# Attention and routed feed-forward on one core: two self iterations in one bank, eleven iterations a unit, pieces in new places

## The chip, the cores and the metric

The kernel runs on one core of a Trainium2 chip. The time is device microseconds of one execution, from its first to its last instruction on the core, with what lies around them. TensorE (PE) multiplies matrices, VectorE (DVE) and ScalarE (ACT) work on 128 partitions, GpSimd (POOL) does light work beside them, SyncE (SP) issues DMAs. The program is written by hand, engine by engine, with semaphores.

## The reference

Eight batches of 512 tokens with 256 channels, and a context of 1024 tokens for each:

```python
scale = np.float32(1.0 / np.sqrt(D))                      # 16 heads of D = 16
q = _heads(x @ Wq + bq); k = _heads(x @ Wk + bk); v = _heads(x @ Wv + bv)
att = jnp.einsum('bhqd,bhkd->bhqk', q, k) * scale
att = jnp.where(causal[None, None], att, -jnp.inf)
y = jnp.einsum('bhqk,bhkd->bhqd', jax.nn.softmax(att, axis=-1), v)
qc = _heads(x @ Wcq + bcq); kc = _heads(cross_input @ Wck + bck); vc = _heads(cross_input @ Wcv + bcv)
attc = jnp.einsum('bhqd,bhkd->bhqk', qc, kc) * scale
y = y + jnp.einsum('bhqk,bhkd->bhqd', jax.nn.softmax(attc, axis=-1), vc)
...
x = x + xattn(_layernorm(x), ctx)
x = x + ffn(_layernorm(x))    # gate, top 512 tokens for each of 8 experts, LN, fc1, gelu, fc2, weight, scatter-add
```

## The kernel before

`attention` computes the first line of the two; `feed_forward`, a second block behind it, the other. The change is in `attention` alone.

**Units and iterations.** A batch has four units (`UNITS`) of four heads. In a unit the scores are computed keys by queries: iterations 0 to 7 (`CROSS_IT`) take one tile of 128 context keys each, against 512 queries; iterations 8 to 11 one tile of 128 own keys each, against the 512, 384, 256 and 128 queries that may see it (`score_span`). For every head of an iteration PE makes scores in a PSUM bank (L577), ACT takes the exponential into `probs` (L784), POOL zeroes the forbidden corner of self tiles (L1084), and PE multiplies by the values into `out_ps` (L593, `values`). `probs` has two buffers, so the values of an iteration are multiplied at the end of the next. When the cross or the self part of a unit is complete, ACT copies `out_ps` out (`copy_out`, L796).

**Maxima.** The softmax shift of a row is its largest score. PE makes the scores a second time, queries by keys (L614), and DVE reduces them: over 512 context keys (L871), or with the causal mask (L874). A unit has 48 of these (`N_A`), four an iteration (`A_PER_IT`), made 68 maxima (`LEAD`) ahead of the unit's scores. `finish_maxima` and the piece "shift" turn them into two rows that are laid beside q by DMA (`put_shift`).

**Two halves of the array.** q and k are kept as high and low parts, stacked: each head uses 64 of the 128 partitions (`SIDE`). Heads 0 and 2 stand in the lower half, 1 and 3 in the upper, so a score matmul of one half can run beside one of the other. Scores go upper, lower (`for side in (1, 0)`), maxima lower, upper by their number.

**Banks.** Three PSUM banks (`SCORE_BANKS`) go round among scores and pieces, four (`RING`) among maxima and the pieces that DVE consumes (`by_vector`: out and proj). PE waits in `bank_free` until the last user of a bank is done.

**Pieces.** All other work of the attention (projections q, qc, k, kc, v, vc of the next batches, transposes, output projection, norm, gate) is cut into pieces. The table `PLAN` says at which (unit, iteration) each stands; PE, ACT, DVE and POOL all walk through the same table. In an iteration PE's order is: maximum, two scores, maximum, pieces, maximum, two scores, maximum, values of the iteration before. For a q, qc, k or kc piece ("half piece", names in `COL`), PE multiplies, ACT writes the rounded high part (L821), DVE subtracts it from the bank for the low part (`low_half`, L929) and so frees the bank, SP stores both to DRAM (`store_parts`) and loads the stacks of a unit from there (`fill`).

**Start.** DVE and POOL clear `q_stack` and `k_stack` (L992, L995, L1001; L1113, L1115), POOL presets `v_self` and `v_cross` (L1116, L1117); DVE normalizes the first tokens (L998), PE transposes them and makes the first ten half pieces, SP fills the stacks of units 0 and 1 directly (`fill_directly`, L462). Then PE and DVE make `LEAD` maxima, and the batches begin.

## Time and profile before

| | us |
|---|---|
| median of 3 runs | 1687.46 (1686.04 to 1691.6) |
| profiled execution, its own time | 1687.51 |
| its span | 1685.8 |
| start, up to the first maximum | 0 to 46.5 |
| first maxima | 46.5 to 88.2 |
| batches with their epilogue | 88.2 to about 1315 |
| feed-forward | about 1315 to 1685.8 |

The span is cut by the first and last instructions of each stage. Within the batches a unit lasts 35 to 41 us, 32 of them stand in a row. Matmul durations overlap: what one costs the engine is the distance of its start to the next start. A group's idle time is that of its own engine; DVE, ACT and POOL have idle time all along the batches, and only such of it counts as ends in a wait of PE.

### The profile page before, as it was taken

To read this page: it belongs to the slowest core of one execution; us is meant where nothing else is said; L and a number is where in the kernel's file an instruction comes from. 1 tells how busy PE (TensorE), PEld (TensorE's weight loads), DVE (VectorE), ACT (ScalarE), POOL (GpSimd) and SP (SyncE) were. 2 spreads that over 40 slices of the span, in tenths; PEclk is the share of its full clock that TensorE was granted. 3 is DMA by queue.
4 is the path that set the end of the run, shared out by engine and by line. 5 is a ranking of instruction groups with operands and counts; after the bars stand their busy time and mean duration, and the time that the engine had idled before them with its cause. 6 is when DMAs were issued, how large, how long until landed. Compare 5 with 4: busy or idle time off the path is not lost. (4 is left out here: it accounts for less than half of the span.)

```text
span 1685.8 us, 26485 instructions
## 1 busy us (share of the span) xinstructions
PE 1524.3 (90%) x8921; PEld 723.5 (43%) x8921; DVE 1190.5 (71%) x3234; ACT 920.4 (55%) x1882; POOL 422.0 (25%) x859
## 2 busy tenths in 40 slices
PE   5799999999999999999999999999999525999997
PEld 2443343444344434444443444334333312665564
DVE  7778887887888788778877887887880165555441
ACT  2067777677766677676777677677767100112111
POOL 4021131322132113212231322131131301343342
PEclk7689999999999999899999999999999656999999
DMA  3673772765285547636671855376200210444432
GB/s 87 155 132 90 131 92 71 110 119 104 79 121 110 95 90 126 112 84 100 120 116 66 122 100 100 89 122 116 34 3 3 70 48 14 116 90 109 116 82 50
DMA packets 82492, 155.47 MB, mean 92 GB/s; under 512 B 13012, under 2 KB 46420, under 8 KB 82356
## 3 DMA queue, kind: packets, MB, share of 16 engines
q1 hardware_dynamic: 76212, 145.25, 44.4%
q0 software_dynamic: 6144, 8.52, 2.9%
q8 instruction: 71, 1.16, 0.3%
q14 instruction: 65, 0.53, 0.1%
HBM read 96.52 MB, written 53.08 MB: 89 GB/s over the span
## 5 line engine op out<-in xcount | busy, mean ns | idle before, releaser
L784 ACT ACTIVATE probs<-bank_ps 128x512 f32<-128x512 f32 (+3 forms) x1536 | 743.3, 545 | 277.9 <-PE bank_ps L577 271.7
L871 DVE TENSOR_REDUCE chunk_max<-bank_ps 128x1 f32<-128x512 f32 x1024 | 646.8, 681 | 88.7 <-PE bank_ps L614 86.3
L577 PE MATMUL bank_ps<-q_stack,k_stack 64*128 64x512 f32 (+3 forms) x1536 | 542.2, 432 | 33.4 <-ACT probs L784 26.8
L614 PE MATMUL bank_ps<-k_stack,q_stack 62*128 62x512 f32 (+3 forms) x1536 | 560.0, 441 | 10.6 <-DMA k_stack<-parts 5.1
L614 PEld LDWEIGHTS bank_ps<-k_stack,q_stack 62*128 62x128 f32 x1536 | 254.0, 190 | 390.1 <-DVE chunk_max L871 177.0
L577 PEld LDWEIGHTS bank_ps<-q_stack,k_stack 64*128 64x128 f32 x1536 | 237.3, 187 | 117.0 <-ACT probs L784 101.1
L593 PE MATMUL out_ps<-probs,v_cross 128*32 128x512 f32 x2048 | 272.7, 605 | 0.0
L874 DVE CUSTOM_DVE_ANT_0 masked<-bank_ps,causal 128x128 bf16<-128x128 f32 (+3 forms) x512 | 232.2, 485 | 30.5 <-PE bank_ps L614 26.5
L1035 POOL TENSOR_TENSOR pool_idle<-pool_idle 128x1 f32<-128x1 f32 x287 | 55.4, 193 | 599.1 <-ACT probs L784 429.7
L1317 ACT ACTIVATE h<-h_ps,b1T 128x512 f32<-128x512 f32 x64 | 44.0, 687 | 269.5 <-PE h_ps L1270 138.5
L1284 PE MATMUL o_ps<-w2T,h 128*128 128x256 f32 x512 | 115.4, 382 | 14.2 <-DVE o L1425 7.2
L1075 POOL TENSOR_TENSOR y_sb<-y_sb,y_add 128x256 f32<-128x256 f32 x32 | 23.3, 728 | 415.1 <-DVE y_add L917 415.1
L1270 PE MATMUL h_ps<-ff_yT,w1T 128*128 128x512 f32 x256 | 122.9, 616 | 1.0 <-DVE ff_yT L1330 1.0
L929 DVE SCALAR_TENSOR_TENSOR parts<-bank_ps,bias,parts 128x512 fp32r<-128x512 f32 x75 | 56.2, 750 | 80.4 <-ACT parts L821 80.2
L1284 PEld LDWEIGHTS o_ps<-w2T,h 128*128 128x128 f32 x512 | 95.5, 190 | 35.5 <-issue 13.3
L1084 POOL TENSOR_SCALAR_AFFINE_SELECT probs<-probs 128x256 f32<-128x256 f32 x256 | 104.2, 407 | 0.0
L593 PE MATMUL out_ps<-probs,v_self 128*32 128x512 f32 (+3 forms) x1024 | 98.0, 457 | 0.0
L821 ACT ACTIVATE parts<-bank_ps,bias 128x512 fp32r<-128x512 f32 x75 | 51.6, 688 | 58.5 <-PE bank_ps L630 54.8
L593 PEld LDWEIGHTS out_ps<-probs,v_cross 128*32 128x32 f32 x2048 | 40.3, 108 | 76.4 <-issue 52.1
L1523 POOL TENSOR_TENSOR ff_pool_idle<-ff_pool_idle 128x1 f32<-128x1 f32 x48 | 12.9, 268 | 213.8 <-DVE index_next L1378 129.5
L1270 PEld LDWEIGHTS h_ps<-ff_yT,w1T 128*128 128x128 f32 x256 | 46.0, 193 | 39.9 <-issue 39.5
L1368 DVE TENSOR_SCALAR onehot<-iota,e_row 128x128 bf16<-128x128 bf16 x256 | 44.3, 253 | 11.6 <-PE list_ps L1258 11.5
(157 smaller groups left out, 1344.5 us busy)
## 6 DMA issues: line engine op xcount, KB each, us to landing
parts_dram<-parts SPq DMA_DIRECT2D x70, 512.0 KB, 2.7
k_stack<-parts_dram SPq DMA_DIRECT2D x180, 192.0 KB, 11.5
q_stack<-parts_dram SPq DMA_DIRECT2D x180, 128.0 KB, 10.5
w1T<-in_L_ffn_fc1s SPq DMA_DIRECT2D x8, 1024.0 KB, 5.7
w2T<-in_L_ffn_fc2s SPq DMA_DIRECT2D x8, 1024.0 KB, 7.3
z_rows<-z_sb SPq DMA_DIRECT2D x8, 528.0 KB, 3.0
x_sb<-in_x SPq DMA_DIRECT2D x8, 512.0 KB, 4.0
ctxT<-in_ctx SPq DMA_DIRECT2D x8, 512.0 KB, 5.3
```

Source lines behind the costliest of these rows:

```text
L577: pe.matmul(bank_of(turn)[:, q0:T], k_stack[base:base + SIDE, g, pair, kc:kc + P], q_stack[base:base + SIDE, g, pair, qc + q0:qc + T], sta ...
L593: mm = pe.matmul(out_ps[32 * h:32 * h + 32, q0:T], v[:, g // 2, kt, g % 2 * UH + h, :], probs[:, i % 2 * 2 + h // 2, h % 2, q0:T], start=k ...
L614: return pe.matmul(bank[:, 0:n], q_stack[base:base + MAX_ROWS, g, pair, qc:qc + P], k_stack[base:base + MAX_ROWS, g, pair, k0:k0 + n], sta ...
L784: nc.scalar.activation(probs[:, i % 2 * 2 + p, side, q0:T], bank_of(("score", g, i, p, side))[:, q0:T], ACT.Exp, scale=SCALE)\
L821: nc.scalar.activation(parts_of(piece)[:, 0], bank[:], ACT.Identity, bias=bias[:, BIAS[name], hf:hf + 1]).then_inc(high_done, 1)
L871: nc.vector.tensor_reduce(dst, bank[:, 0:n], AX.X, ALU.max).then_inc(max_done, 1)
L874: nc.vector.tensor_tensor_reduce(masked[:, a % 2, 0:n], bank[:, 0:n], causal[:, T - n:T], 1.0, LOWEST, ALU.add, ALU.max, dst).then_inc(max ...
L929: nc.vector.scalar_tensor_tensor(out=parts_of(piece)[:, 1], in0=bank[:], scalar=bias[:, BIAS[name], hf:hf + 1], in1=parts_of(piece)[:, 0], ...
L1035: nc.gpsimd.tensor_tensor(pool_idle[:, c:c + 1], pool_idle[:, 0:1], pool_idle[:, 0:1], ALU.add)
L1084: nc.gpsimd.affine_select(out=tile, in_=tile, pattern=[[0, 2], [1, P]], compare_op=ALU.is_ge, fill=0.0, base=0, channel_multiplier=-1).the ...
L1270: mm = pe.matmul(h_ps[:, f % 2], w1T[:, k, f * P:(f + 1) * P], yT[:, k, :], start=k == 0, stop=k == KT - 1)
L1284: mm = pe.matmul(o_ps[:, t % 2, 0:C], h[:, f, t * P:(t + 1) * P], w2T[:, f, :], start=f == 0, stop=f == FT - 1)
```

## The change

- The last two self tiles, 256 and 128 queries wide, share a bank (`score_spans`): two score matmuls per head, one exponential over 384 columns, both masks behind it. A unit has 11 iterations (`ITS`), the last is the joined one.
- The 48 maxima of a unit stand as 4 in iterations 0 to 6 and 5 in 7 to 10 (`A_AT`). With five, three stand ahead of the pieces and two behind (`ahead_of_pieces`).
- `probs` gets a third pair of buffers; PE multiplies the values of an iteration two iterations later (`BEHIND`), ACT's `copy_out` moves one iteration back.
- Half pieces of batches 1 to 7 (70 of 80): ACT writes the unrounded value once, which frees the bank (`whole_done`); POOL rounds a copy and subtracts it (`split_halves`). DVE's part goes. SP waits for POOL (`halves_ready`).
- `PLAN` is rewritten: shift in iteration 7, not 8; k, kc0, kc1, qc, q, gate and others one to three iterations away from where they stood.
- Start: DVE clears the last three quarters of `q_stack` behind the normalization, in one; POOL clears the rest of `k_stack` only when the normalization is done; pair 0 of unit 0 is filled with q and k before pair 1; six warm-up matmuls, not four.

```diff
-ITS = 12
-A_PER_IT = 4
-N_A = ITS * A_PER_IT
+SELF_ITS = 3
+ITS = CROSS_IT + SELF_ITS
+A_AT = (4, 4, 4, 4, 4, 4, 4, 5, 5, 5, 5)
+A_FROM = tuple(itertools.accumulate(A_AT, initial=0))
+N_A = A_FROM[ITS]
...
+BEHIND = 2
+PROB_BUFFERS = BEHIND + 1
...
-    (2, 6): (("vc0", 0),), (2, 8): (("shift", 0),), (2, 9): (("qc", 1),), (2, 11): (("k", 1),),
+    (2, 6): (("vc0", 0),), (2, 7): (("shift", 0),), (2, 8): (("qc", 1),), (2, 10): (("k", 1),),
...
-            for pair in range(UH // SIDES):
-                fill_directly(0, pair, True, first_in[pair])
+            fill_directly(0, 0, True, first_in[0])
             sp.wait_ge(*freed(prologue_piece(PROLOGUE.index(("kc1", 0)))))
-            for pair in range(UH // SIDES):
-                fill_directly(0, pair, False, first_in[pair])
+            fill_directly(0, 0, False, first_in[0])
+            fill_directly(0, 1, True, first_in[1])
+            fill_directly(0, 1, False, first_in[1])
...
+            if i < ITS - 1:
+                return [self_span(i - CROSS_IT, (i - CROSS_IT) * P)]
+            return [self_span(SELF_ITS - 1, 0), self_span(SELF_ITS, T - (SELF_ITS - 1) * P)]
...
                         maxima(0)
                         score_pair(b, g, i, 0, first, last)
-                        maxima(1)
+                        for n in range(1, ahead_of_pieces(i)):
+                            maxima(n)
...
-                        maxima(2)
+                        maxima(A_AT[i] - 2)
                         score_pair(b, g, i, 1, first, last)
-                        maxima(3)
-                        if not (first and g == 0 and i == 0):
-                            values(*before)
+                        maxima(A_AT[i] - 1)
+                        done = ITS * (UNITS * b + g) + i - BEHIND
+                        if done >= 0:
+                            values(done // (ITS * UNITS), done // ITS % UNITS, done % ITS)
...
-                    nc.scalar.activation(parts_of(piece)[:, 0], bank[:], ACT.Identity,
-                                         bias=bias[:, BIAS[name], hf:hf + 1]).then_inc(high_done, 1)
+                    if piece.of > 0:
+                        nc.scalar.activation(parts_of(piece)[:, 1].bitcast(F32), bank[:], ACT.Identity,
+                                             bias=bias[:, BIAS[name], hf:hf + 1]).then_inc(whole_done, 1)
...
-                elif piece.name in COL:
+                elif piece.name in COL and piece.of == 0:
                     low_half(piece, bank)
...
-            nc.vector.memset(q_stack[:, 1].bitcast(F32), 0.0).then_inc(q_clear, 1)
             dve.wait_ge(rstd_step[0], 2)
...
-            nc.vector.memset(q_stack[:, 2:4].bitcast(F32), 0.0).then_inc(q_clear, 1)
+            nc.vector.memset(q_stack[:, 1:4].bitcast(F32), 0.0).then_inc(q_clear, 1)
...
+            def split_halves(piece):
+
+                a, e = COL[piece.name]
+                n = number_of(piece) - 2 * len(HALF_PIECES) + 1
+                pool.wait_ge(whole_done, n)
+                hold()
+                nc.gpsimd.tensor_copy(parts[:, 0, a:e], parts[:, 1, a:e].bitcast(F32)).then_inc(rounded, 1)
+                pool.wait_ge(rounded, n)
+                nc.gpsimd.tensor_tensor(parts[:, 1, a:e], parts[:, 1, a:e].bitcast(F32), parts[:, 0, a:e].bitcast(F32),
+                                        ALU.subtract).then_inc(split_done, 1)
...
             deviation(0, 1)
+            pool.wait_ge(ln_done[0], 1)
             nc.gpsimd.memset(k_stack[:, 1:4].bitcast(F32), 0.0).then_inc(k_clear, 1)
```

**SP at the start**, the direct fills of units 0 and 1; before:

```order
17 L425 DMA gateT<-in_L_ffn_gate_w 128x16
18 L462 DMA q_stack<-parts 16x1024 x12
19 L462 DMA k_stack<-parts 16x1536 x12
20 L462 DMA q_stack<-parts 16x1024 x6
21 L462 DMA k_stack<-parts 16x1536 x6
```

and now:

```order
17 L447 DMA gateT<-in_L_ffn_gate_w 128x16
18 L484 DMA q_stack<-parts 16x1024 x6
19 L484 DMA k_stack<-parts 16x1536 x6
20 L484 DMA q_stack<-parts 16x1024 x6
21 L484 DMA k_stack<-parts 16x1536 x6
```

Six q fills, those of pair 1, have moved behind the six k fills of pair 0.

**PE at the end of unit 3**, from values to values; L614 are maxima, L577 scores, L593 values. Before, the 128-wide iteration, with its two scores of each pair between maxima:

```order
1109 L593 MATMUL out_ps<-probs,v_self 32x384 x4
1110 L614 MATMUL bank_ps<-k_stack,q_stack 128x384
1111 L577 MATMUL bank_ps<-q_stack,k_stack 128x128 x2
1112 L614 MATMUL bank_ps<-k_stack,q_stack 128x384
1113 L614 MATMUL bank_ps<-k_stack,q_stack 128x512
1114 L577 MATMUL bank_ps<-q_stack,k_stack 128x128 x2
1115 L614 MATMUL bank_ps<-k_stack,q_stack 128x512
1116 L593 MATMUL out_ps<-probs,v_self 32x256 x4
```

and now the joined one (L655 maxima, L616 scores, L634 values):

```order
1117 L655 MATMUL bank_ps<-k_stack,q_stack 128x512
1118 L616 MATMUL bank_ps<-q_stack,k_stack 128x256
1119 L616 MATMUL bank_ps<-q_stack,k_stack 128x128
1120 L616 MATMUL bank_ps<-q_stack,k_stack 128x256
1121 L616 MATMUL bank_ps<-q_stack,k_stack 128x128
1122 L655 MATMUL bank_ps<-k_stack,q_stack 128x384 x2
1123 L655 MATMUL bank_ps<-k_stack,q_stack 128x512
1124 L616 MATMUL bank_ps<-q_stack,k_stack 128x256
1125 L616 MATMUL bank_ps<-q_stack,k_stack 128x128
1126 L616 MATMUL bank_ps<-q_stack,k_stack 128x256
1127 L616 MATMUL bank_ps<-q_stack,k_stack 128x128
1128 L655 MATMUL bank_ps<-k_stack,q_stack 128x512
```

A fifth maximum has come in, and each head has two score matmuls in a row on its half of the array.

**POOL around the first half pieces of a batch** (unit 0 into unit 1), before:

```order
193 L1035 TENSOR_TENSOR pool_idle<-pool_idle 128x1
194 L1084 AFFINE_SELECT probs<-probs 128x2x128
195 L1075 TENSOR_TENSOR y_sb<-y_sb,y_add 128x4x64
196 L1035 TENSOR_TENSOR pool_idle<-pool_idle 128x1
197 L1084 AFFINE_SELECT probs<-probs 128x2x128
```

and now:

```order
217 L1081 TENSOR_TENSOR pool_idle<-pool_idle 128x1
218 L1142 AFFINE_SELECT probs<-probs 128x2x128 x2
219 L1081 TENSOR_TENSOR pool_idle<-pool_idle 128x1
220 L1129 CAST parts<-parts 128x512
221 L1131 TENSOR_TENSOR parts<-parts 128x512
222 L1081 TENSOR_TENSOR pool_idle<-pool_idle 128x1
223 L1129 CAST parts<-parts 128x512
224 L1131 TENSOR_TENSOR parts<-parts 128x512
```

Between the masks of a unit and its `y_sb` addition POOL now has a copy and a subtraction for each half piece.

## Rows read from the trace of the kernel before

**Rows 1.** The page, part 1: busy us, share of the span, instructions.

```profile
PE 1524.3 (90%) x8921; PEld 723.5 (43%) x8921; DVE 1190.5 (71%) x3234; ACT 920.4 (55%) x1882; POOL 422.0 (25%) x859
```

**Rows 2.** Engines by stretch: length, then busy us of each, PEclk, DMA.

```profile
88.20:1315.00 1226.80, 1187.85 (x7527) 510.32 (x7527) 953.91 (x2372) 861.05 (x1795) 287.87 (x690) 0.98 0.53 95
```

**Rows 3.** Timeline, DVE at the start: start us, us, instruction, count, idle before.

```profile
8.71 13.58 DVE L998 TENSOR_SCALAR x_sb<-x_sb,mean_var,rstd 128x256 f32<-128x256 f32 x4
```

**Rows 4.** Line L998 alone: durations ns min/median/max.

```profile
L998 DVE TENSOR_SCALAR x_sb<-x_sb,mean_var,rstd x4: 395/400/12619, 8.7 to 21.9; 128x256 f32<-128x256 f32 x4
```

**Rows 5.** Timeline, POOL at the start.

```profile
8.22 7.77 POOL L1115 MEMSET k_stack<- 128x9216 f32 x1
...
17.67 3.50 POOL L1117 MEMSET v_cross<- 128x4096 f32 x1
```

**Rows 6.** Timeline, PE at the start.

```profile
22.43 1.94 PE L625 MATMUL bank_ps<-ident,x_sb 128*128 128x128 f32 x8 [15.11 <-DVE x_sb L998]
25.14 3.75 PE L630 MATMUL bank_ps<-y0T,w_q 128*128 128x512 f32 x4 [0.77 <-ACT y0T L813]
28.69 2.39 PE L630 MATMUL bank_ps<-y0T,w_cq 128*128 128x512 f32 x4
30.91 1.88 PE L630 MATMUL bank_ps<-y0T,w_k 128*128 128x512 f32 x4
...
46.48 0.51 PE L614 MATMUL bank_ps<-k_stack,q_stack 62*128 62x512 f32 x1 [5.10 <-DMA k_stack<-parts]
```

**Rows 7.** Timeline, SP's DMA issues at the start.

```profile
32.69 7.58 SPq L462 DMA_DIRECT2D q_stack<-parts  x12
40.31 7.55 SPq L462 DMA_DIRECT2D k_stack<-parts  x12
```

**Rows 8.** Timeline, PE in batch 4, unit 2: iteration 2 (w_q) and iteration 3 (no piece).

```profile
792.79 0.50 PE L614 MATMUL bank_ps<-k_stack,q_stack 62*128 62x512 f32 x1
...
793.45 1.06 PE L593 MATMUL out_ps<-probs,v_cross 128*32 128x512 f32 x8
794.45 0.50 PE L614 MATMUL bank_ps<-k_stack,q_stack 62*128 62x512 f32 x1
...
795.73 0.49 PE L577 MATMUL bank_ps<-q_stack,k_stack 64*128 64x512 f32 x1 [0.21 <-ACT probs L784]
...
796.15 1.07 PE L593 MATMUL out_ps<-probs,v_cross 128*32 128x512 f32 x8
```

**Rows 9.** Timeline, all engines behind a q piece, batch 4, unit 0 into unit 1.

```profile
744.20 0.69 ACT L821 ACTIVATE parts<-bank_ps,bias 128x512 fp32r<-128x512 f32 x1 [1.49 <-PE bank_ps L630]
744.92 0.75 DVE L929 SCALAR_TENSOR_TENSOR parts<-bank_ps,bias,parts 128x512 fp32r<-128x512 f32 x1 [1.53 <-ACT parts L821]
745.20 0.49 PE L614 MATMUL bank_ps<-k_stack,q_stack 62*128 62x512 f32 x1
745.82 0.50 PE L577 MATMUL bank_ps<-q_stack,k_stack 64*128 64x512 f32 x2
```

**Rows 10.** Timeline, PE in batch 3, unit 2, iteration 8 (shift, then late scores).

```profile
652.63 0.50 PE L614 MATMUL bank_ps<-k_stack,q_stack 62*128 62x512 f32 x1
653.13 0.99 PE L577 MATMUL bank_ps<-q_stack,k_stack 64*128 64x512 f32 x2
...
654.04 1.06 PE L593 MATMUL out_ps<-probs,v_cross 128*32 128x512 f32 x8
```

**Rows 11.** Timeline, POOL in batch 4, unit 2.

```profile
801.79 1.22 POOL L1053 TENSOR_SCALAR z_sb<-x,mean_var,rstd 128x256 f32<-128x256 f32 x1
803.09 2.37 POOL L1068 TENSOR_TENSOR x<-x,z_sb 128x1024 f32<-128x1024 f32 x1
```

**Rows 12.** Timeline, DVE at that time.

```profile
802.76 2.47 DVE L871 TENSOR_REDUCE chunk_max<-bank_ps 128x1 f32<-128x512 f32 x4
```

**Rows 13.** Engines by stretch, at the starts of batches 3 and 2.

```profile
548.30:554.50 6.20, 6.20 (x32) 4.08 (x31) 3.72 (x8) 3.75 (x7) 0.00 (x0) 0.50 0.75 152
394.00:400.20 6.20, 6.20 (x50) 3.57 (x49) 4.87 (x10) 5.14 (x10) 0.00 (x0) 1.00 0.75 163
```

More of the change, by code:

```diff
@@ L371, in bank_of, with buffer @@
             return bank_ps[:, SCORE_TURNS.index(turn) % SCORE_BANKS]
+        def buffer(u, i, pair):
+            return (ITS * u + i) % PROB_BUFFERS * 2 + pair
         def parts_of(piece):
@@ L430, in store_parts @@
                 a, e = COL[name]
[L431 removed]
+                sp.wait_ge(*halves_ready(piece))
                 if stacked and name == HALF_PIECES[0]:
```

107 lines of the change are left out of this document (65 added, 42 removed), and 13 rows, old and new, of the table PLAN.

## The prediction

> **What bounds the kernel now.** I read the busy shares first: PE is busy for 90% of the span, DVE for 71% [rows 1]. Then the stretches: the batches take 1226.8 us, and PE is busy for 1187.9 of them, at a granted clock of 0.98; DVE for 953.9, ACT for 861 [rows 2]. So the batches go by PE. But "busy" counts waiting in the pipeline as well, so the timeline has to say how much of it is work. It gives a price to each part of an iteration, from start to start: two maxima with two scores 0.66 us (792.79 to 793.45), four 512-wide value products 1.00 us (793.45 to 794.45) [rows 8]. An iteration without a piece is then worth 0.66 + 0.66 + 1.00 = 2.32 us, but takes 2.70 (793.45 to 796.15, values to values): 0.39 us stand in its second half, where the fourth score waits for ACT, since only three banks go round [rows 8]. This is a chain of latencies (score, exponential, bank), not anyone's load. The change leaves that chain as it is: three banks, same order.
>
> Such stalls can be counted through the batch. I find four kinds. (a) Behind a half piece DVE stands 1.53 us waiting for ACT's high part and then works 0.67 on the low part; PE has made one maximum at 745.20 and can go on only at 745.82, 0.6 us late [rows 9]. There are five such places a batch (behind q, qc, k of half 1, kc0, kc1), 2.8 us. (b) In the shift iteration the second half starts at 652.63 and the values at 654.04, 1.41 us where 0.66 would do [rows 10]: 0.75, four a batch, 3.0 us. (c) The iterations 9 to 11 wait some 0.2 to 0.4 each, 2.8 us a batch. (d) Iterations of context keys with no piece in a score or ring bank, 0.39 each [rows 8]; seven a batch.
>
> The start has bounds of its own. The first normalization on DVE takes 13.58 us for four small operations [rows 3]: the median of them is 0.40, one lasts 12.62 [rows 4]. It ends when POOL's last memset does: those run from 8.22 to 21.17 without a gap that matters [rows 5]. PE waits for it for 15.11 us [rows 6].
>
> **The change, part by part.**
>
> *Start.* (1) POOL's memsets wait for the normalization. It then costs 4 x 0.4 and begins at about 8.3: it ends near 10.0 and not at 22.3, a gain of 12.3 [rows 3, 4]. The Trainium skill (SBUF — State Buffer, Who interferes with whom) has this as a lock which the one that issues first holds for the whole instruction; the trace has the wait through three memsets in a row, not one, and the sum is the same by both. (2) q and qc took 3.75 and 2.39 where k took 1.88 [rows 6], because PE had stood idle; with six warm-up matmuls and a gap of about 1 us the clock should be at its upper level: 2.3 less. The last half piece of the start ends at about 26.9 instead of 41.4. (3) SP may begin the direct fills when `k_stack` is clear: 10.0 + 7.77 [rows 5] = 17.8, where it began at 32.69 [rows 7]. Pair 0 now needs six q issues (half of 7.58) and six k issues (half of 7.55) [rows 7]: 17.8 + 7.6 = 25.4, and 2.8 for the landing (from the issue at 40.31 + 3.4 to the first maximum at 46.48 [rows 6, 7]): 28.2. Both PE and DVE are done with the pieces by then. The first maximum moves from 46.48 to about 28.3: **-18 us**. DVE runs the maxima behind it at its own pace, so all of it stays. Ends: if PE gets the lower clock for all ten half pieces (3.75 each as the first one), the fills are no longer what ends last, and 10 are left; -19 if the first maxima also run smoother.
>
> *Half pieces.* DVE's wait and work (2.2 us, 70 times) go, and ACT's one write frees the bank. The stalls (a) go: -2.8 a batch. ACT's part costs what it did. POOL gets a copy and a subtraction of 512 columns. No row shows such a copy; memset gives the lower end (7.77 / 9216 x 512 = 0.4 us [rows 5]), the two-operation form the upper (1.22 for 256 columns [rows 11], 2.4). The subtraction is 2.37 / 2 = 1.2 [rows 11]. So 1.6 to 3.6 us, say 2.6, ten times in 152 us, on an engine busy for 288 of 1227 us [rows 2]. The masks stand behind it in POOL's queue; their consumer on PE now comes two iterations later, 5 us and more. SP's stores come 2 to 4 us later, while the fill with the least slack (half 0 into unit 0's stacks) has some 12 us between its landing and its first maximum. Price: 0, as long as that cover holds.
>
> *Eleven iterations.* The number of scores and maxima by columns is the same; an iteration's overhead goes. ACT saves four exponentials a unit, but is not the bound. The stalls (c) go with the sparse iterations 9 to 11, and shift (b) comes to an iteration with five maxima, so that PE works where it waited: -5.8 a batch. Two pieceless iterations of (d) are filled: -0.8. Against it: in an iteration with five maxima the alternation of the halves breaks. Before, a maximum and a score of different halves always go together, 0.33 us for both [rows 8]. Now one maximum stands alone, and at odd numbers (28 + 5 = 33) maximum and first score are on the same half. I count two unpaired slots a unit more than before: 8 x 0.336 = +2.7 a batch. The joined iteration has two score matmuls of one half behind each other, +0.4 a unit, +1.6. Pieceless self iterations still have the chain (d): four at 0.35, +1.4. `copy_out` now waits for values of 256 and 128 columns (0.57 + 0.36 us) instead of 128 alone: half of 0.57 shows, +1.1. Five reductions of 0.6 (2.47 for four [rows 12]) against an iteration of 2.9 to 3.2: +0.8. Sum: -9.4 + 7.6 = -1.8 a batch, **-14.4 us** for eight. The two values products left at the end cost +0.6.
>
> What same-half neighbours cost is not in this trace, since it has none. The nearest rows bound it: 0 if they overlap as opposite halves do, 0.336 if they do not at all [rows 8]. I take the upper end, since a pair starts in the same 0.01 us and the next pair only 0.34 later. The Trainium skill speaks against the change here (TensorE: Matmul & The Clock Gate, Part 3, The mechanism): the weight load runs beside matmuls in flight only if the row group differs. By it the +2.7 stand; by the other end the batches would gain 4.5 each.
>
> *Third buffer, values two behind.* PE waits for no mask or exponential ahead of its values now that would be worth a term, so this gives 0 by itself. It is the cover for POOL's new work.
>
> *Sum.* 1687.5 (the profiled execution, and the median to 0.1) - 18.0 - 14.4 + 0.6 = **1655.7 us**. The span would be 1654.
>
> **The rivals.**
>
> *R1, the halves do overlap, or the chain (d) shrinks where five maxima stand.* Then +2.7 and +1.4 fall away: 1656 - 8 x 3 = 1632 to 1640. For it: POOL and ACT have room. The clock works the same way: at the starts of batches 3, 4 and 5 it fell to the lower level for about 10 us. Beside the start of batch 2, 32 matmul records stand there instead of 50 in 6.2 us [rows 13]; the three falls cost about 6.5 us together. Ahead of them PE has sparse iterations (9 to 11 of unit 3), and these are denser now. Against it: the gate piece, eight-column matmuls, stays there.
>
> *R2, the batches gain nothing.* The new stalls (copy behind values, five reductions, unpaired slots) eat all 9.4: 1687.5 - 18 = 1669. For it: I have 7.6 of them from bounds, and at several places the values to values distance is PE's work already. The start stands by itself.
>
> *R3, the other side: slower.* POOL's split holds DVE. For the start the trace shows that DVE can stand for the whole of a POOL instruction [rows 3, 5]. If every split stopped the maxima for 2.6 to 3.6 us, against a slack of DVE in such an iteration of 4.0 - 4 x 0.6 = 1.6, this costs 1 to 2 us for each of 70: 1656 + 70 to 140 = 1726 to 1796, slower than before from 0.5 us a split upwards. Against it: while POOL runs 1.22 and 2.37 us operations that read and write SBUF, DVE's four maxima take 2.47 us as everywhere [rows 11, 12].
>
> *R4, the start gains less*, -10, with the batches as forecast or flat: 1664 to 1678.
>
> **How the numbers follow.** Forecast (1648 to 1663) 0.42, R1 0.23, R2 0.19, R4 0.10, R3 0.03, and 0.03 for something of another kind on the slow side. The predicted time is that of the forecast, 1656. From 1636 to 1676 it takes in forecast, most of R1, R2 and half of R4: about 0.8. About 0.3% (5 us) can be told from no change: faster than 1682.4 is 0.92; within 0.3% 0.04 (R4 with batches that lose 5 us); slower 0.04.
>
> **What would show each step.** Start: L998's successor at 0.4 us each, the first maximum at 28 to 29 us, first scores at about 70 instead of 88. If it is at 36, the clock of the half pieces was low. Batches: their stretch 1212 us instead of 1227. The five places (a): the score behind a maximum follows at once. Unpaired slots: in iterations 7 to 9, a maximum starting 0.33 us behind the other matmul of its half. The shift iteration at 3.2 us, as before, but full. POOL's copy and subtraction at 0.4 to 2.4 and 1.2 us, and maxima on DVE at 0.6 us apart beside them; if they stretch, R3 is right. I am wrong altogether if a fill lands late and PE waits for `slot_in` at the first maxima of a unit, or if the clock falls at many unit starts: each fall costs 2 to 3 us.

## The result and the profile after

The changed kernel takes 1622.4 us (median of 4 runs, 1616.12 to 1627.09), the kernel before 1689.23 beside it (4 runs). The ratio is 0.9603, with a 95% interval of 0.9565 to 0.9641: 67 us faster, where 32 had been forecast (1656, range 1636 to 1676). The sign was right, the size was not, and the time lies below the range.

The page after, part 1, answers to [rows 1]; behind it, in a fence of its own, the stretch of the batches (columns as in [rows 2]).

```profile
PE 1486.5 (92%) x8925; PEld 726.8 (45%) x8925; DVE 1135.0 (70%) x3163; ACT 911.5 (56%) x1754; POOL 550.1 (34%) x1005
```

```profile
69.10:1252.00 1182.90, 1153.28 (x7523) 516.38 (x7523) 909.74 (x2300) 852.30 (x1667) 415.87 (x836) 0.99 0.56 99
```

POOL has 128 us more to do than before, DVE 56 less, and PE's busy time has shrunk by 38 with about as many matmuls (8925 for 8921 [rows 1]): most of that is waiting inside PE's pipeline that has gone, since busy time counts it. By the first and the last exponential of the attention I cut both traces into three: the first exponential comes at 70.0 us where it came at 89.1 (-19.1), the batches from there to the last exponential take 1178.8 us where they took 1221.9 (-43.1), and what lies behind takes 372.9 where it took 374.8 (-1.9). The forecast had -18, -14.4 and +0.6. The batches are what was missed.

The start went as planned. Timeline of DVE, PE and SP there; the rows answer to [rows 3, 6, 7]:

```profile
8.35 1.38 DVE L1044 TENSOR_SCALAR x_sb<-x_sb,mean_var,rstd 128x256 f32<-128x256 f32 x4 [1.64 <-POOL rstd L1090]
11.75 3.55 PE L671 MATMUL bank_ps<-y0T,w_q 128*128 128x512 f32 x4 [0.82 <-ACT y0T L856]
15.14 1.88 PE L671 MATMUL bank_ps<-y0T,w_cq 128*128 128x512 f32 x4
18.63 3.78 SPq L484 DMA_DIRECT2D q_stack<-parts  x6
28.93 0.47 PE L655 MATMUL bank_ps<-k_stack,q_stack 62*128 62x512 f32 x1 [1.61 <-DVE u_sb L976]
```

The normalization takes 1.38 us instead of 13.58, the fills begin at 18.63, the first maximum stands at 28.93. What released it is DVE's last low half, not a fill.

POOL's new work in the middle of a batch (batch 4, unit 2 into unit 3), a copy and a subtraction of one half piece; behind it DVE's maxima in the same time, and the durations (ns, min/median/max) of all DVE maxima over 512 context keys:

```profile
777.73 0.61 POOL L1129 CAST parts<-parts 128x512 fp32r<-128x512 f32 x1
778.42 1.29 POOL L1131 TENSOR_TENSOR parts<-parts 128x512 fp32r<-128x512 f32 x1
```

```profile
777.27 1.29 DVE L918 TENSOR_REDUCE chunk_max<-bank_ps 128x1 f32<-128x512 f32 x2 [0.36 <-PE bank_ps L655]
```

```profile
L918 DVE TENSOR_REDUCE chunk_max<-bank_ps x1024: 656/681/694, 29.4 to 1200.2; 128x1 f32<-128x512 f32 x171
```

The copy takes 0.61 us, the subtraction 1.29. DVE's two maxima beside the copy take 1.29 us, half of the 2.47 for four in [rows 12], and none of the 1024 lasts longer than 0.694 us, though 70 copies and 70 subtractions stand among them. R3, POOL holding DVE, did not happen, though the start of the kernel before had shown a DVE operation standing through POOL's memsets [rows 4, 5]. The Trainium skill (SBUF — State Buffer, Who interferes with whom) tells the two apart: it names tensor_scalar, the normalization's operation, as one that can contend with GpSimd, and tensor_reduce, the maxima's, as one that never does on trn2. Both rows agree.

### The profile page after: what moved, and what is told of

It reads as the page before. It is cut to its first block and busy times, and to the rows that moved or that the text cites. A ratio compares the mean times of both kernels' runs of the same rounds, so it can differ in the third digit from the quotient of the medians.

```text
span 1621.7 us, 26374 instructions
## 1 busy us (share of the span) xinstructions
PE 1486.5 (92%) x8925; PEld 726.8 (45%) x8925; DVE 1135.0 (70%) x3163; ACT 911.5 (56%) x1754; POOL 550.1 (34%) x1005
## 5 line engine op out<-in xcount | busy, mean ns | idle before, releaser
L827 ACT ACTIVATE probs<-bank_ps 128x512 f32<-128x512 f32 (+1 forms) x1408 | 730.4, 579 | 247.2 <-PE bank_ps L616 238.5
L918 DVE TENSOR_REDUCE chunk_max<-bank_ps 128x1 f32<-128x512 f32 x1024 | 653.5, 683 | 143.4 <-PE bank_ps L655 139.6
L655 PE MATMUL bank_ps<-k_stack,q_stack 62*128 62x512 f32 (+3 forms) x1536 | 536.1, 432 | 7.7 <-DVE chunk_max L918 4.4
L616 PE MATMUL bank_ps<-q_stack,k_stack 64*128 64x512 f32 (+3 forms) x1536 | 511.7, 422 | 26.0 <-ACT probs L827 22.6
L655 PEld LDWEIGHTS bank_ps<-k_stack,q_stack 62*128 62x128 f32 x1536 | 248.2, 191 | 371.3 <-DVE chunk_max L918 201.6
L634 PE MATMUL out_ps<-probs,v_cross 128*32 128x512 f32 x2048 | 274.3, 608 | 0.0
L616 PEld LDWEIGHTS bank_ps<-q_stack,k_stack 64*128 64x128 f32 x1536 | 234.5, 189 | 83.9 <-ACT probs L827 76.5
L1131 POOL TENSOR_TENSOR parts<-parts 128x512 fp32r<-128x512 f32 x70 | 89.3, 1276 | 5.6
L634 PE MATMUL out_ps<-probs,v_self 128*32 128x512 f32 (+3 forms) x1024 | 90.4, 449 | 0.1
L634 PEld LDWEIGHTS out_ps<-probs,v_cross 128*32 128x32 f32 x2048 | 40.3, 108 | 76.7 <-issue 48.1
L865 ACT ACTIVATE parts<-bank_ps,bias 128x512 f32<-128x512 f32 x70 | 48.2, 689 | 46.6 <-PE bank_ps L671 43.5
L1612 POOL DMA_INDIRECT out<-o,index x32 | 50.7, 1584 | 5.2 <-issue 5.2
```

The costliest lines, as they stand in the source:

```text
L616: mm = pe.matmul(bank_of(turn)[:, of.at:of.end], k_stack[base:base + SIDE, g, pair, of.keys:of.keys + P], q_stack[base:base + SIDE, g, pai ...
L634: mm = pe.matmul(out_ps[32 * h:32 * h + 32, of.q0:T], v[:, g // 2, of.tile, g % 2 * UH + h, :], probs[:, buffer(u, i, h // 2), h % 2, of.a ...
L655: return pe.matmul(bank[:, 0:n], q_stack[base:base + MAX_ROWS, g, pair, qc:qc + P], k_stack[base:base + MAX_ROWS, g, pair, k0:k0 + n], sta ...
L827: nc.scalar.activation(probs[:, buffer(u, i, p), side, columns], bank_of(("score", g, i, p, side))[:, columns], ACT.Exp, scale=SCALE)\
L918: nc.vector.tensor_reduce(dst, bank[:, 0:n], AX.X, ALU.max).then_inc(max_done, 1)
L1131: nc.gpsimd.tensor_tensor(parts[:, 1, a:e], parts[:, 1, a:e].bitcast(F32), parts[:, 0, a:e].bitcast(F32), ALU.subtract).then_inc(split_don ...
```

## The experiments

The kernel before ran beside every group of them, at medians of 1686.5 to 1689.2 us. "Forecast" is the prediction's own theory; further theories are named where they came up.

Each median holds two things: how long the iterations last, and how long PE's granted clock was at the lower of its two levels. To tell them apart I add up a batch from the trace of each kernel: for every (unit, iteration) the time from its first maximum to that of the next iteration, as the median over batches 1 to 6 of those that lie outside the stretches at the lower clock. The last column has the time at the lower clock between 100 us and the last exponential. Both come from one execution of each kernel.

| kernel | median, us | a batch at the upper clock, us | at the lower clock, us |
|---|---|---|---|
| before | 1689.2 | 153.8 | 28.9 |
| start alone | 1669.3 | 153.8 | 6.2 |
| POOL's split alone | 1679.3 | 152.0 | 40.5 |
| changed, without the split | 1634.4 | 149.2 | 27.3 |
| changed, twelve iterations, old places | 1655.8 | 151.3 | 37.6 |
| twelve iterations, new places | 1652.1 | 151.4 | 20.5 |
| twelve iterations, old places, 5, 5, 3, 3 maxima | 1666.9 | 152.9 | 27.9 |
| twelve iterations, 5, 5, 3, 3, sides matched | 1662.7 | 151.5 | 40.1 |
| **changed** | 1622.4 | 147.8 | 20.5 |
| changed, old places | 1617.6 | 147.5 | 20.5 |
| changed, sides matched | 1608.5 | 146.8 | 0 |
| changed, sides crossed | 1689.4 | 155.8 | 37.5 |
| sides matched, four score banks | 1634.9 | 149.6 | 13.7 |

**The start alone.** The start's edits on the kernel before.

```diff
-WARM_UP = 4
+WARM_UP = 6
...
-            nc.vector.memset(q_stack[:, 1].bitcast(F32), 0.0).then_inc(q_clear, 1)
...
+            pool.wait_ge(ln_done[0], 1)
             nc.gpsimd.memset(k_stack[:, 1:4].bitcast(F32), 0.0).then_inc(k_clear, 1)
```

> The kernel before with the start of the changed kernel alone (memsets behind the normalization, pair 0 filled first, six warm-up matmuls). Theory A (the start is worth what the forecast worked out, 18 us, and all of it stays): 1689 - 18 = 1671 us, first scores near 70 instead of 89, unit periods as before. Rival B (an earlier start also changes where the clock falls in the batches): the periods of units change by some us, and the time is 5 us or more off 1671.

Measured: 1669.29 us, ratio 0.9886 (0.9861 to 0.9911): -19.9. The start is worth its 18, which lie within the interval, and R4 is out. The first exponential starts at 69.95 us, 19.2 earlier than before; the units behind are as before, with less time at the lower clock in the profiled execution.

**POOL's split alone.** ACT writes the whole value, POOL makes the halves; all else as before.

```diff
-                    nc.scalar.activation(parts_of(piece)[:, 0], bank[:], ACT.Identity,
-                                         bias=bias[:, BIAS[name], hf:hf + 1]).then_inc(high_done, 1)
+                    if piece.of > 0:
+                        nc.scalar.activation(parts_of(piece)[:, 1].bitcast(F32), bank[:], ACT.Identity,
+                                             bias=bias[:, BIAS[name], hf:hf + 1]).then_inc(whole_done, 1)
...
```

> The kernel before with the half pieces of batches 1 to 7 split by POOL alone, everything else as before. Theory A (the forecast's term: 0.6 us of PE stall behind five half pieces a batch, 2.8 us a batch): 1689 - 20 = 1669 us. Theory B (the part that was under-sized is this one, because DVE's 2.2 us per half piece also delays the maxima of the iterations behind it): 5 us a batch, 1689 - 35 = 1654 us. Theory C (POOL's masks come late behind the split with only two probs buffers): no gain, 1685 to 1695.

**And the changed kernel without it**, DVE making the low half again.

```diff
-                elif piece.name in COL and piece.of == 0:
+                elif piece.name in COL:
                     low_half(piece, bank)
```

> The changed kernel with the half pieces split by ACT and DVE as before. Theory A: 1622 + 20 = 1642 us. Theory B (the split is the larger part): 1622 + 35 = 1657 us. If less than 10 us is lost, the new places of the half pieces already hide DVE's part.

Measured: 1679.26 us, 0.9945 (0.9926 to 0.9964) for the split alone, -9.9; 1634.37 us, 0.9670 (0.9642 to 0.9697) without it, 12.0 more than the changed kernel. The forecast had 22.4; the expectation's 20 was too much as well, and neither of its rivals fits. Timeline of PE behind the q piece of the kernel with the split alone (batch 4, into unit 1), the place of [rows 9]:

```profile
738.60 0.50 PE L623 MATMUL bank_ps<-k_stack,q_stack 62*128 62x512 f32 x1
738.60 0.74 PE L586 MATMUL bank_ps<-q_stack,k_stack 64*128 64x512 f32 x2
...
743.98 0.49 PE L586 MATMUL bank_ps<-q_stack,k_stack 64*128 64x512 f32 x1 [0.47 <-ACT probs L793]
```

The scores start with their maximum, where 0.62 us had stood between them [rows 9]: the stall (a) is gone there. But in the next iteration PE waits 0.47 us for an exponential. The list of waits shows how much of this there is (us in total, times, longest), first before, then with the split alone:

```profile
PE bank_ps L577 <- ACT probs L784: 26.8, 86, 0.8
```

```profile
PE bank_ps L586 <- ACT probs L793: 33.0, 100, 0.8
```

6.2 us of the gain come back as waits for exponentials. That is half of what the forecast had too much. By place, at the upper clock, a batch gains 1.8 us and not 2.8: 0.58 each in iteration 0 of units 1 and 3, 0.30 and 0.09 in the iterations behind them, and 0.2 in unit 2; the forecast had five places of nearly 0.6. Seven batches have the split, which makes 12 us by place; the trace has 40.5 us at the lower clock where the kernel before had 28.9, and that takes some of it back.

**Twelve iterations again.** The changed kernel with its start, split and third buffer, but with twelve iterations, four maxima in each, and the pieces where they stood.

```diff
-SELF_ITS = 3
+SELF_ITS = 4
...
-A_AT = (4, 4, 4, 4, 4, 4, 4, 5, 5, 5, 5)
+A_AT = (4,) * ITS
```

> The changed kernel with twelve iterations and four maxima each again, pieces where they stood before (v and out_cross of unit 0 exchanged, since the values run two iterations behind); start, split and third probs buffer stay. Theory A (joining and five maxima give what the forecast did not see: its costs of 7.6 us a batch are mostly not there): 1622 + 23 = 1645 us. Theory B (the split is the larger part): 1622 + 8 = 1630 us.

Measured: 1655.84 us, 0.9794 (0.9767 to 0.9822), 33.4 more than the changed kernel. By the forecast it should have been eight us faster than the changed kernel. So here is the step that failed: the eleven iterations were booked as a small loss and are half of the whole gain. What is left for the third buffer on the way there is a remainder, not a measurement: 1689.2 - 19.9 - 9.9 - 3.5 = 1655.9, and - 33.4 = 1622.5.

**Places or joining?** Two kernels take "fewer iterations" and "new places" apart: twelve iterations with the new places, and eleven with the old ones. The first against the kernel with twelve iterations and old places, in part; the second goes the other way, as far as eleven iterations allow:

```diff
-    (0, 5): (("vc1", 1),), (0, 6): (("yT0", 0),), (0, 7): (("yT1", 0),), (0, 8): (("shift", 0),),
...
+    (0, 5): (("vc1", 1),), (0, 6): (("yT0", 0),), (0, 7): (("shift", 0),), (0, 8): (("yT1", 0),),
...
-    (2, 6): (("vc0", 0),), (2, 8): (("shift", 0),), (2, 9): (("qc", 1),), (2, 11): (("k", 1),),
+    (2, 6): (("vc0", 0),), (2, 7): (("shift", 0),), (2, 8): (("qc", 1),), (2, 10): (("k", 1),),
```

> The kernel with twelve iterations and four maxima each (its start, split and third buffer are the changed kernel's), but with the pieces where the changed kernel has them: shift in iteration 7, k in (1, 1), kc0 in (1, 3), qc half 1 in (2, 8), gate in (3, 9). With the old places it took 1655.8, the changed kernel 1622.4. Theory A: the 33.4 us between them come from the joined iteration and the fives that go with it, the new places being only what eleven iterations need; then this kernel stays within 5 us of the old places: 1651 to 1661. Theory B: the new places spread PE's waits (the shift a step ahead of the self iterations, half pieces apart from each other) and bring a third or more: 1645 or less, down to 1622 if they bring all.

> The changed kernel, joined iteration and fives, but with the pieces where they stood before, as far as eleven iterations allow (shift in iteration 8, k in (1, 2), kc0 and kc1 in (1, 6) and (1, 7), qc half 1 in (2, 9); the pieces of iteration 11 in 10, gate in (3, 9)). Theory A, joining and fives bring the 33.4 us: within 5 us of the changed kernel, 1617 to 1627. Theory B, the new places bring a third or more: 1633 to 1656. There is less time between shift and the first scores of the next unit here (two iterations and a half instead of three and a half), so that PE could wait for the fill at every unit start: then the kernel is slower for that reason, and the waits on DMA at the first scores show it.

Measured: 1652.07 us, 0.9793 (0.9771 to 0.9815), against 0.9794 with the old places; and 1617.59 us, 0.9589 (0.9572 to 0.9607), against 0.9603 with the new. The places are worth nothing that can be told in either kernel: theory A both times. The joining with its fives brings 0.019 to 0.021 at either set of places.

**The fives without the joining.** Twelve iterations, old places, but 5, 5, 3 and 3 maxima in the self iterations.

```diff
-A_AT = (4,) * ITS
+A_AT = (4,) * CROSS_IT + (5, 5, 3, 3)
```

> The unjoined twelve-iteration kernel (1655.8 us) with 5, 5, 3, 3 maxima in the four self iterations instead of 4 each. Theory A (the gain of the joined version comes mostly from filling the shift iteration, where PE waits 0.75 us, with a maximum from the narrow ones): 1656 - 15 = 1641 us or less. Theory B (it comes mostly from the joining itself: one iteration less): 1650 us or more.

Measured: 1666.92 us, 0.9874 (0.9846 to 0.9903), 11 more than with four each. Maxima taken from the sparse iterations to the fuller ones are no gain, they cost (theory B). By place, at the upper clock, the two iterations with five last 0.21 to 0.25 us longer each, and the two with three give back 0.25 in one unit of four and 0.05 at most elsewhere. So it is the joining that pays and not the moving; what the joining would be worth without its fives has no run.

The lists of waits agree. PE's waits for a score bank, in which an exponential is still being read: twelve iterations with four maxima each, the same at the new places, twelve with 5, 5, 3, 3, and the changed kernel.

```profile
PE bank_ps L614 <- ACT probs L825: 28.8, 98, 0.8
```

```profile
PE bank_ps L614 <- ACT probs L825: 26.6, 81, 0.8
```

```profile
PE bank_ps L614 <- ACT probs L825: 38.7, 123, 0.9
```

```profile
PE bank_ps L616 <- ACT probs L827: 22.6, 66, 0.7
```

From the first to the last 32 waits and 6.2 us are gone; 17 of them go with the new places alone, which bring no time, and 15, or 4.0 us, with the joining. What one unit gains shows in the timeline of PE, batch 4, unit 2. First twelve iterations: iterations 10 (one bank each for 256 queries) and 11 (128 queries), from values to values.

```profile
784.30 0.50 PE L653 MATMUL bank_ps<-k_stack,q_stack 62*128 62x512 f32 x1
...
785.37 0.38 PE L614 MATMUL bank_ps<-q_stack,k_stack 64*128 64x256 f32 x1 [0.21 <-ACT probs L825]
...
785.80 1.06 PE L632 MATMUL out_ps<-probs,v_self 128*32 128x512 f32 x8
786.79 0.44 PE L653 MATMUL bank_ps<-k_stack,q_stack 62*128 62x384 f32 x1
...
787.28 1.98 PE L669 MATMUL bank_ps<-y0T,w_k 128*128 128x512 f32 x4
789.19 0.50 PE L653 MATMUL bank_ps<-k_stack,q_stack 62*128 62x512 f32 x1
...
789.73 0.85 PE L632 MATMUL out_ps<-probs,v_self 128*32 128x384 f32 x8
```

Then the joined iteration of the changed kernel:

```profile
772.34 0.50 PE L655 MATMUL bank_ps<-k_stack,q_stack 62*128 62x512 f32 x1
...
773.17 1.98 PE L671 MATMUL bank_ps<-y0T,w_k 128*128 128x512 f32 x4
775.09 0.50 PE L655 MATMUL bank_ps<-k_stack,q_stack 62*128 62x512 f32 x1
...
775.74 1.07 PE L634 MATMUL out_ps<-probs,v_self 128*32 128x512 f32 x8
```

Iterations 10 and 11 take (785.80 - 784.30) + (787.28 - 786.79) + (789.73 - 789.19) = 2.53 us for their scores and eight maxima. The joined one takes 0.83 + 0.65 = 1.48 for the same score columns and five maxima. The three other maxima cost about 0.22 each in iterations 7 to 9 (a half with three maxima and two scores takes 0.89 us, one with two and two 0.67). That leaves 2.53 - 1.48 - 0.66 = 0.39 us in this unit, where the forecast had booked the joined scores at a loss of 0.4.

One unit is not the mean. The cleanest pair for that are the two kernels at the new places: same pieces, and 20.5 us at the lower clock in both. A batch takes 151.4 us with twelve iterations and 147.8 in the changed kernel: 3.6 a batch, times eight 28.7, where the medians lie 29.7 apart. Of the 3.6, the maxima and scores from iteration 7 on give 1.5, with the fives paid. The values give 0.7: those of the two tiles take 0.79 us together where they took 0.57 + 0.36 apart. The maxima and scores of iterations 0 to 6 give 1.1, nearly all of it in iteration 2; why there, I can't say. The pieces, with the waits at them, give 0.3. At the old places the same sum has 3.5 a batch, 28 of the 33.4; that kernel has 37.6 us at the lower clock and the changed one 20.5, which at half speed is up to 8.5 more.

The shift iteration is no part of the gain. In units 0 to 2 it does its fifth maximum for 0.09 us (2.04 us of maxima and scores against 1.95), but in unit 3, where it has two pieces, it lasts 4.22 us against 3.62.

**The sides of scores.** If a maximum and a score of one half of the array stand behind each other, do they cost 0.336 us, as forecast, or nothing? Two kernels change only in which order the two scores of a pair are given out: in one ("matched") the first score of a pair is always on the other half than the maximum ahead of it, in the other ("crossed") always on the same half.

```diff
-                for side in (1, 0):
+                for side in side_order(i, p):
...
+def side_order(i, p):
+    ahead = A_FROM[i] + (A_AT[i] - 2 if p else 0)
+    return (1, 0) if ahead % SIDES == 0 else (0, 1)
```

> The changed kernel; where a pair of scores follows a maximum of the upper half (iterations 7, 8, 9 and 10, once each), the scores go lower, upper and not upper, lower, so that neighbours are on opposite halves everywhere. Theory A (the forecast's term: a same-half neighbour costs a slot of 0.33 us, two a unit): 1622 - 20 = 1602 us. Theory B (the trace of the changed kernel: a group with a fifth maximum lasts 0.89 us, one with four 0.67, so the extra one costs 0.22 and the neighbour nothing): within 5 us of 1622.

The crossed kernel has the two results of `side_order` exchanged.

> The changed kernel with the scores of every pair in the order that puts the first one on the same half of the array as the maximum ahead of it, so two same-half neighbours in every group of four (32 x 22 groups). Theory A (a same-half neighbour costs a slot of 0.33 us): at least 0.33 us a group, 1622 + 230 = 1850 us. Theory B (it costs nothing or some 0.05 us): 1622 to 1660 us.

Measured: 1608.48 us, 0.9540 (0.9515 to 0.9566) with the sides matched, 13.9 less than the changed kernel: **this version beats both kernels**. Crossed: 1689.36 us, 1.0006 (0.9991 to 1.002), 81 more than matched. The matched kernel has four crossed pairs of scores a unit fewer than the changed one, 128 in all, the crossed one 22 a unit more than the matched one, 704: 0.11 us each from both medians. Neither theory had that number. The agreement is in part the clock's: at the upper clock the batches differ by 1.0 us (0.07 a pair) and 9.0 (0.10, or a little less: two of the 44 iterations lie at the lower clock in every batch of the crossed trace, and stand in the sum with their shortest time). So of the 13.9 us some 8 are the order itself; the rest goes with the clock, which is at its lower level for 20.5 us in the changed kernel and for none in the matched one. The timeline shows why one price is the wrong form. PE in batch 4, unit 2, iteration 4, matched:

```profile
742.13 0.50 PE L666 MATMUL bank_ps<-k_stack,q_stack 62*128 62x512 f32 x1
742.13 0.73 PE L627 MATMUL bank_ps<-q_stack,k_stack 64*128 64x512 f32 x2
...
742.80 0.66 PE L677 MATMUL bank_ps<-ident,u_sb 128*128 128x128 f32 x4
743.38 0.50 PE L666 MATMUL bank_ps<-k_stack,q_stack 62*128 62x512 f32 x1
743.39 0.73 PE L627 MATMUL bank_ps<-q_stack,k_stack 64*128 64x512 f32 x2
...
744.06 1.07 PE L645 MATMUL out_ps<-probs,v_cross 128*32 128x512 f32 x8
```

The same, crossed:

```profile
788.96 0.50 PE L666 MATMUL bank_ps<-k_stack,q_stack 62*128 62x512 f32 x1
788.97 0.73 PE L627 MATMUL bank_ps<-q_stack,k_stack 64*128 64x512 f32 x2
...
789.64 0.66 PE L677 MATMUL bank_ps<-ident,u_sb 128*128 128x128 f32 x4
790.22 0.49 PE L666 MATMUL bank_ps<-k_stack,q_stack 62*128 62x512 f32 x1
790.45 0.50 PE L627 MATMUL bank_ps<-q_stack,k_stack 64*128 64x512 f32 x2
...
791.12 1.06 PE L645 MATMUL out_ps<-probs,v_cross 128*32 128x512 f32 x8
```

The first half takes 0.67 us in one and 0.68 in the other, though its pairs are crossed there: as a group the matmuls lose nothing. The second half takes 0.68 and 0.90: its first score starts 0.23 behind the maximum and not with it. It is so throughout: over the 24 units of batches 1 to 6, iteration 4 has medians of 0.67 and 0.67 us for the first half, 0.67 and 0.89 for the second. ACT's exponentials tell what happened between, matched and crossed:

```profile
742.75 1.08 ACT L838 ACTIVATE probs<-bank_ps 128x512 f32<-128x512 f32 x2 [0.64 <-PE bank_ps L627]
```

```profile
789.80 1.09 ACT L838 ACTIVATE probs<-bank_ps 128x512 f32<-128x512 f32 x2 [0.96 <-PE bank_ps L627]
```

The first exponential starts 0.62 us after the first maximum in one (742.13 to 742.75) and 0.84 in the other (788.96 to 789.80); the medians over those units are 0.63 and 0.83. The crossed order delivers the first score 0.22 us later, and the chain score, exponential, bank, with three banks, hands this on to the second half. Where a long piece stands between the halves (w_cq, w_k, 1.91 us from start to start), the second half takes 0.67 in both kernels. So such a neighbour costs 0.2 where that chain ends last, and nothing where it doesn't. For the engine alone the forecast's lower end, 0, was the right one. The Trainium skill (TensorE: Matmul & The Clock Gate, Part 3, The mechanism) has the weight load of the same row group wait for the matmul ahead; the first half of 0.68 us shows that this needn't lengthen a group, and the exponential 0.22 us later that it does delay a result.

**Matched sides without the joining.** Does matching give the same with twelve iterations and 5, 5, 3, 3?

```diff
-                for side in (1, 0):
+                for side in side_order(i, p):
```

> The twelve-iteration kernel with 5, 5, 3, 3 maxima in the self iterations (u_moved, 1666.9 us), with the scores on opposite halves to the maxima ahead of them everywhere. Theory A (a same-half neighbour costs 0.11 us, u_moved had four a unit, and filling the shift iteration is worth little by itself): 1667 - 14 = 1653 us, as a_unjoined (1655.8). Theory B (filling the waits of the shift iteration was worth something, but something else than neighbours slowed u_moved): 1645 us or less, or no change from 1667.

Measured: 1662.70 us, 0.9854 (0.9826 to 0.9883), 4.2 less, and the intervals overlap; theory A had 14 less. At the upper clock, though, theory A is right: a batch takes 151.5 us, as with four maxima each (151.3), where 5, 5, 3, 3 with crossed pairs took 152.9. The shift iteration gains 0.23 us, and some others 0.1. The clock hides it, being at its lower level for 40.1 us against 27.9. So at the upper clock the fives cost nothing but their crossed sides.

**A fourth bank for scores.** If the chain is the limit, another score bank should help; it has to come from the ring of the maxima.

```diff
-SCORE_BANKS = 3
-RING = 4
+SCORE_BANKS = 4
+RING = 3
```

> The changed kernel with scores in the order of a_sides (1608.5 us), four banks for scores and three for maxima. Theory A (what is left of PE's waits is the chain of latencies over three score banks): iterations without a piece fall from 2.70 to about 2.35 us, shift iterations from 3.16 to about 2.8, some 4 us a batch, 1608 - 30 = 1578 us. Theory B (three banks for maxima make PE wait for DVE instead): 1608 us or more, with PE's waits for chunk_max grown.

Measured: 1634.89 us, 0.9685 (0.9655 to 0.9715), 26 more than with the sides matched and three banks: theory B. The list of PE's waits, three banks and four, first for a bank with an exponential, then for a bank with a maximum:

```profile
PE bank_ps L627 <- ACT probs L838: 19.9, 61, 0.7
PE bank_ps L666 <- DVE chunk_max L929: 4.2, 8, 1.1
```

```profile
PE bank_ps L627 <- ACT probs L838: 4.1, 12, 0.6
PE bank_ps L666 <- DVE chunk_max L929: 20.2, 69, 2.1
```

Both sides are real. The waits for exponentials fall from 61 to 12, so the chain over three banks was a limit; the waits for maxima rise from 8 to 69. By place, seven of the 44 iterations of a batch get shorter by 0.1 us and more, but fourteen get longer by 0.15 to 0.6, six of the nine without a piece among them.

**The third buffer.** Values one iteration behind, two buffers of `probs`.

```diff
-BEHIND = 2
+BEHIND = 1
```

> The changed kernel with the values one iteration behind and two pairs of probs buffers, as before the change. Theory A (the forecast: PE waits for no mask or exponential worth a term, the third buffer is only a cover): within 5 us of 1622. Theory B (the values two behind carry a part of the gain that the forecast did not see, since masks stand behind POOL's splits and the joined iteration's four masks take 1.9 us): 1622 + 10 to 30 us.

Measured: 1628.71 us, 0.9657 (0.9633 to 0.9681), 6.3 more, where 0 was forecast; the intervals overlap. The two profiled executions are 1.0 us apart (1624.4 and 1623.4), and a batch at the upper clock takes 148.2 us against 147.8: some 3 us in eight. More than that has no place in the traces.

**The narrow tile itself.** What is left in the 128-query tile? On top of matched sides, this kernel leaves out the last self tile, its scores, masks and values, and so computes something else.

```diff
-            return [self_span(SELF_ITS - 1, 0), self_span(SELF_ITS, T - (SELF_ITS - 1) * P)]
+            return [self_span(SELF_ITS - 1, 0)]
```

> The changed kernel with scores in the order of a_sides (1608.5 us), and the 128-wide self tile left out: its score matmuls, masks and value products are gone, the joined iteration keeps its exponential over 384 columns and its five maxima. It measures what the second tile costs inside the joined iteration. Theory A (the forecast's prices: 0.4 us a unit for second score matmuls on the same half, 0.36 for the values): 0.76 x 32, 1608 - 24 = 1584 us. Theory B (by the trace of the changed kernel: the values of the joined iteration last 0.79 us where 256 columns alone lasted 0.57, the scores hardly more than alone): 0.22 to 0.32 us a unit, 1608 - 7 to 10 = 1598 to 1601 us.

Measured: 1606.28 us, 0.9513 (0.9492 to 0.9534), 2.2 less than with it. Work was taken away, and hardly any time. At the upper clock a batch takes 145.6 us against 146.8: 0.43 us less in two units of four and less in the others, some 10 us in eight batches. The timeline of PE at the end of a unit 3 (batch 5), behind the gate piece, with the tile and without it:

```profile
943.60 1.95 PE L682 MATMUL bank_ps<-gateT,zT 128*128 128x8 f32 x16
...
946.09 1.07 PE L645 MATMUL out_ps<-probs,v_cross 128*32 128x512 f32 x8
947.09 0.50 PE L666 MATMUL bank_ps<-k_stack,q_stack 62*128 62x512 f32 x1
```

```profile
944.05 1.64 PE L647 MATMUL out_ps<-probs,v_cross 128*32 128x512 f32 x8
945.62 0.79 PE L668 MATMUL bank_ps<-k_stack,q_stack 62*128 62x512 f32 x1
...
947.91 1.93 PE L647 MATMUL out_ps<-probs,v_self 128*32 128x512 f32 x8
949.78 0.79 PE L668 MATMUL bank_ps<-k_stack,q_stack 62*128 62x512 f32 x1
```

The stretch view for that place without the tile, columns as in [rows 2]:

```profile
944.90:950.90 6.00, 6.00 (x27) 2.56 (x23) 3.50 (x9) 2.48 (x7) 1.64 (x6) 0.50 0.65 210
```

The granted clock is 0.50 there, the lower level, and the values take 1.57 and 1.87 us instead of 1.00. The kernel with the tile has no such fall behind its first 100 us; this one has six, 23.9 us together, all at the end of a unit 3. They take most of the 10 us back: in batches 1 to 6 the iterations at the lower clock last 7 us longer than their places do at the upper. What brings the falls I can't tell: the gate piece, eight-column matmuls, stands ahead of them in both kernels.

## Why the prediction was right and wrong

**Start: right.** 18 forecast, 19.9 measured alone. The normalization at 0.35 us each, the first maximum at 28.93 (28.3), the first scores at 69.1 (70). Two parts were wrong: q and qc took 3.55 + 1.88, not 2 x 1.88, so the clock gave 0.7 us and not 2.3, and DVE's low halves ended last instead of the fills. Together they made the first maximum 0.6 us late.

**Half pieces (a): right in kind, twice too large.** 22.4 forecast, 9.9 alone and 12.0 in the changed kernel. The term was five stalls of nearly 0.6 us a batch. Two places gave 0.58, the others 0.1 to 0.3; I hadn't asked what is late next behind them. It is the exponential, with 6.2 us of new waits.

**Eleven iterations: this step failed.** It stood at -5.8 - 0.8 + 7.6 = +1.0 us a batch, +8 in all, and measured -33.4, or -4.2 a batch. At the upper clock it is -3.6 a batch. Both sides of the sum were off, the side "against" most, since it priced chains and neighbours from bounds and not by what the same work had cost before:

- Unpaired slots, +2.7 a batch: taken from the upper end of a range of 0 to 0.336. The matched kernel shows 13.9 us for them, 1.7 a batch, of which 1.0 is there at the upper clock, and by another way: not PE's slots, but a score that is late for its exponential.
- Joined scores, +1.6: two narrow tiles in two iterations each had a second half that waited, with too few columns beside it. The maxima and scores from iteration 7 on, fives included, need 1.5 a batch less, not more. I had counted the joined matmuls' handicap and not the one that they had before. The same holds for the values, -0.7 a batch, and for iteration 2, -1.1, which had no term.
- Chain in pieceless self iterations, +1.4: there was as much of it before. PE's waits for exponentials fell, from 98 to 66, or from 81 at the same places.
- `copy_out`, +1.1: no cost. The maxima and scores of iteration 2 of unit 1, behind it, take 1.76 us in batch 4, and 2.22 with twelve iterations at the same places.
- Five reductions, +0.8: nothing. The list of PE's waits has 4.4 us behind DVE's maxima in 8 times, as much as the kernel before had in 11:

```profile
PE bank_ps L655 <- DVE chunk_max L918: 4.4, 8, 1.4
```

- Of the side "for", the shift (b) was not there: 3.0 a batch forecast. Its second half still takes 1.15 us and more; it carries a fifth maximum for less in three units, and loses that in the fourth.

**Third buffer: 0 forecast, 6.3 measured.** Its sign is in doubt by the intervals, but a price of 0 "by itself" was argued from waits alone.

**The sum.** Measured against forecast, by pieces: start -1.9, split +12.5, third buffer -3.5 (the remainder on the way over the kernel with twelve iterations), joining -42 with the +0.6 at the end. That makes -35: the 67 measured less the 32 forecast. It closes because the 3.5 is a remainder.

**The rivals.** R1 said that the halves overlap or that the chain shrinks, 1632 to 1640, with 0.23. Both hold in part, and it was nearer than the forecast, but still too slow. Its own two terms are 2.7 + 1.4 = 4.1 a batch and not 3, which would have given 1623; that this is the measured time is luck, since neither term went to 0 and the gain came from others. R2 and R4 are out by the kernels with the start alone and with twelve iterations. R3 is out by the rows of DVE beside POOL. The range should have gone lower: 7.6 us a batch of costs came from bounds, and their lower ends, 0 each, give 8 x 7.6 = 61 us less, of which I had let some 24 into R1.

## What to carry to other kernels

Where an engine loses time in a chain through another one's buffers, count the passes through the chain and not the columns: two thin iterations made into one full one took 3.6 us off a batch, for the same work. Book a term at what the same work costs before the change, not at what it would cost without handicaps; costs that are all taken from upper bounds add up to a bias. When neighbouring work can be given out in either order, put first what can run beside the work ahead of it, if another engine waits for the result; here that brought 14 us, 8 of them at the upper clock. And when an edit brings less or more than its places in the trace, look at the granted clock before explaining the rest.

## What the runs showed of the hardware

- A DVE operation of 0.40 us was held for 12.62 us through three POOL memsets in a row, but beside POOL's copies and subtractions of 0.61 and 1.29 us no maximum that reads PSUM took longer than 0.694.
- Maximum and score of the same half of the array in a row cost a group of four 0.01 us or less, and delayed the first exponential by 0.2 (0.63 to 0.83 behind the group's start).
- Two column-tiled value products of 256 and 128 columns in a row took 0.79 us, apart 0.57 + 0.36.
- Taking some 10 us of work from PE brought 2.2, since the granted clock fell at six places where it hadn't before. Behind the first 100 us the batches have 0 us at the lower level with matched sides, 20.5 in the changed kernel and 37.6 with twelve iterations at the old places, most of it at the end of unit 3; what decides it is open.
